# Two graph-convolution passes whose sum banks carry 128 columns into the next bank, instead of cutting tiles in two

## The reference: what is computed

```python
def gcn_conv(x, src, dst, ew, W, b):
    deg = segment_sum(ew, dst); dinv = where(deg > 0, rsqrt(deg), 0)
    h = x @ W
    msg = h[src] * (dinv[src] * ew * dinv[dst])[:, None]
    return segment_sum(msg, dst) + b
h = relu(gcn_conv(x, ..., W1, b1)); h = sigmoid(gcn_conv(h, ..., W2, b2))
x = layernorm(x + h)
z = x @ fc_w.T; rh = edge_attr @ fc_r_w.T
e = leaky_relu(z[src] @ aw0 + z[dst] @ aw1 + rh @ aw2)
alpha = segment_softmax(e, dst)
out = layernorm(x + relu(segment_sum(alpha * (z[src] + rh), dst) + z @ loop_w))
```

## Time and profile before

| what | value |
|---|---|
| median of 3 runs | 2682.67 us (2680.21 to 2683.11) |
| profiled execution | 2688.04 us, its span 2686.2 us |
| PE / DVE / ACT / POOL busy | 73% / 64% / 9% / 74% of the span |
| granted clock of PE, mean | 0.81 of full speed |
| pass 0 gathers | 5.7 to 843.1 us |
| pass 1 gathers | 856.5 to 1619.8 us |
| pass 2 gathers | 1646.3 to 2640 us |

### The profile page before, as it was taken

How to read it: one execution, slowest core, us unless ns; L and a number is a source line. 1 busy time by engine, 2 the same in 40 slices (tenths; PEclk the granted TensorE clock), 3 DMA queues, 4 the chain that set the end, 5 groups by cost and what they waited for, 6 DMA issues and landing times.

```text
span 2686.2 us, 39490 instructions
## 1 busy us (share of the span) xinstructions
PE 1962.5 (73%) x13505; PEld 1689.4 (63%) x13505; DVE 1731.3 (64%) x7072; ACT 253.3 (9%) x444; POOL 1998.3 (74%) x1973
## 2 busy tenths in 40 slices
PE   5777888989896787979797884466457566567558
PEld 4567767777785565757575763366456556456557
DVE  8989976867764456665656564556556457556465
ACT  0010000101100011101111111000000000000000
POOL 7777777777776777777777774777777777777772
PEclk9659888989986889889878885678788777788777
DMA  4243222222224233343424334644444444444441
GB/s 133 57 118 96 64 70 65 77 63 77 69 65 126 63 83 115 89 123 91 117 78 116 89 107 138 173 116 114 106 113 114 103 114 106 113 114 106 103 104 33
DMA packets 251443, 263.33 MB, mean 98 GB/s; under 512 B 41630, under 2 KB 195765, under 8 KB 251222
## 3 DMA queue, kind: packets, MB, share of 16 engines
q0 software_dynamic: 62784, 130.31, 19.8%
q1 hardware_dynamic: 175214, 123.97, 15.8%
q10 hardware_dynamic: 13240, 6.45, 0.8%
HBM read 247.25 MB, written 13.72 MB: 97 GB/s over the span
## 4 chain that ended last, share of the span: by engine, by line
POOL 45%; issue 19%; PE 16%; DVE 11%; DMA 7%; SPq 1%; ACT 0%; POOLq 0%; DVEq 0%; ACTq 0%
POOL ring L562 45%; PE ps L694 7%; DMA ring<-x_d,srcC 5%; DVE SR L1226 5%; PE ps L749 5%; DVE SR L1257 2%; PE ps L697 1%; DMA ring<-h_d,srcC 1%; PE ps L737 1%; DMA U<-dlo_d 1%; PE ps L679 1%; SPq L400 1%; SPq L482 1%; PE ps L634 0%; DVE SR L1323 0%
## 5 line engine op out<-in xcount | busy, mean ns | idle before, releaser
L562 POOL DMA_INDIRECT ring<-x_d,srcC x1260 | 1262.1, 1002 | 411.4 <-issue 395.2
L694 PE MATMUL ps<-SR,ring 128*128 128x128 f32 (+9 forms) x5076 | 904.3, 311 | 203.1 <-DVE SR L1257 75.3
L694 PEld LDWEIGHTS ps<-SR,ring 128*128 128x128 f32 x5076 | 797.9, 227 | 231.8 <-issue 140.5
L562 POOL DMA_INDIRECT ring<-h_d,srcC x558 | 593.5, 1064 | 183.1 <-issue 175.5
L749 PE MATMUL ps<-SR 128*128 128x376 f32 x1176 | 430.2, 518 | 33.6 <-ACT SR L989 33.6
L697 PE MATMUL ps<-SR 128*128 128x128 f32 (+10 forms) x1948 | 427.4, 305 | 0.0
L697 PEld LDWEIGHTS ps<-SR 128*128 128x128 f32 x1948 | 348.8, 224 | 0.0
L749 PEld LDWEIGHTS ps<-SR 128*128 128x128 f32 x1176 | 233.5, 207 | 176.1 <-ACT SR L989 35.4
L1323 DVE TENSOR_SCALAR SR<-iota_s,cols 128x376 f32<-128x376 f32 x588 | 246.7, 473 | 67.8 <-PE ps L749 67.5
L1257 DVE TENSOR_SCALAR SR<-iota_s,rankC,ewC 128x128 f32<-128x128 f32 x1036 | 280.0, 363 | 0.3
L829 PE MATMUL ps<-ident,cols 128*32 128x128 f32 (+2 forms) x78 | 20.4, 396 | 316.5 <-DVE cols L1533 316.5
(11 more groups left out here) (226 smaller groups left out, 1721.3 us busy)
## 6 DMA issues: line engine op xcount, KB each, us to landing
SR<-in_edge_attr_dram SPq DMA_DIRECT2D x97, 512.0 KB, 4.2
U<-dlo_d SPq DMA_DIRECT2D x98, 256.0 KB, 3.5
ring<-x_d,srcC POOLq DMA_INDIRECT x1260
SR<-low_d SPq DMA_DIRECT2D x72, 256.0 KB, 3.3
ring<-h_d,srcC POOLq DMA_INDIRECT x558
U<-lo_d SPq DMA_DIRECT2D x18, 256.0 KB, 3.2
x_d<-U SPq DMA_DIRECT2D x12, 264.0 KB, 4.5
rows<-x_d SPq DMA_DIRECT2D x12, 264.0 KB
```

What stands on the lines that cost most here:

```text
L562: pool.indirect_dma_start(ring[:, gg % R, k, 0:width], None, (x if p == 0 and h < R0 else table)[:, :], bass.IndirectOffsetOnAxis(ap=srcC[ ...
L694: last = nc.tensor.matmul(ps[(p * NK + k) % 2][:, lo:hi], ring[:, gg % R, j, 0:D], S[:, gg % NS, j, w0:w0 + hi - lo], start=False, stop=t ...
```

## The change

In passes 0 and 1 a bank now owns BA = 384 nodes (three blocks), and there are NA = 17 banks. A bank still has 512 columns. A tile is summed whole into the one bank that `bank_of` names, and columns 384 to 511 hold what its tiles add to the first 128 nodes of the next bank. When a bank has been copied to SBUF, `layer` first adds those 128 columns into the next bank, by one matmul with the identity, and then multiplies the bank's three blocks by the weights. The next bank's first tile is always the first tile of a group (`OPENS`); the last bank, which owns only block 48, is opened inside `layer`. Pass 2 keeps its 13 banks and `pieces`. The sets move to other banks and other groups: those that POOL leaves out in pass 0 were 42-45, 58-61, 74-77, 82-85, 90-93 and are now 44-47, 56-59, 74-77, 80-83, 92-95. Their number stays, as does the number of gathers in each pass.

The core of the diff; elsewhere `NK` becomes `NA`, `blocks(k)` becomes `home(k)` and `CLOSE` becomes `CLOSES` wherever passes 0 and 1 are meant, in the loads of `h1_d`, `x2_d` and `x` (17 smaller DMAs each instead of 13), in `hide`, `squash`, `hidden`, `hidden2`, `normal`, `dst_scores`, `node_table` and `picks_at`.

```diff
+BA = 3 * P
+NA = -(-NP // BA)
+def bank_of(t):
+    return max((GT * t - 2 * (W // 4)) // BA, 0) if t >= GT else 0
+def home(k):
+    return range(k * BA // P, min((k + 1) * BA // P, NB))
+def column(t):
+    return base(t) - bank_of(t) * BA
+OPENS = [min(t for t in range(T) if bank_of(t) == k) for k in range(NA)]
+CLOSES = [max(t for t in range(T) if bank_of(t) == k) // GT for k in range(NA)]
-SETK = (5, 7, 9, 10, 11, 1, 3)
+SETK = (7, 9, 12, 13, 15, 2, 4)
-SAT = [4 * k * P // GT + 16 for k in SETK]
+SAT = [OPENS[k] + GT for k in SETK]
...
 (sum_group)
+                    if p < 2:
+                        k = bank_of(t)
+                        if t == OPENS[k] and k + 1 < NA:
+                            open_bank(p, k)
+                        last = nc.tensor.matmul(ps[(p * NA + k) % 2][:, column(t):column(t) + W], ring[:, gg % R, j, 0:D], S[:, gg % NS, j, :],
+                                                start=False, stop=t + 1 in OPENS or t + 1 == T)
+                        continue
...
 (add_sets)
-                        at = base(SAT[RUNS[i]]) - k * BW
+                        at = column(SAT[RUNS[i]])
...
 (layer)
                 pe.wait_ge(s("evacd"), gb + 1)
+                if k + 2 == NA:
+                    open_bank(p, NA - 1)
+                if k + 1 < NA:
+                    nc.tensor.matmul(ps[(gb + 1) % 2][:, 0:BW - BA], ident[:, :], aggT[:, gb % 2, BA:BW], start=False, stop=False)
                 if gb:
                     pe.wait_ge(s("l_free"), gb)
-                for j, b in enumerate(blocks(k)):
+                for j, b in enumerate(home(k)):
...
 (evacuate)
-                n = len(blocks(k)) * P
+                n = BW if k + 1 < NA else len(home(k)) * P
```

More of the change, by code:

```diff
@@ L77 @@
 CLOSE = [t // GT for t in LAST[0]]
-SETK = (5, 7, 9, 10, 11, 1, 3)
+BA = 3 * P
[8 more added lines that the diff above has]
+CLOSES = [max(t for t in range(T) if bank_of(t) == k) // GT for k in range(NA)]
+assert all(0 <= column(t) and column(t) + W <= BW for t in range(T)) and all(OPENS[k] // GT == CLOSES[k - 1] + 1 for k in range(1, NA))
+SETK = (7, 9, 12, 13, 15, 2, 4)
 USED = ((0, 1, 2, 3, 4), (5, 6, 0, 1, 2, 3, 4))
@@ L90 @@
 SEQ = [(p, q) for p in range(3) for q in GL[p]]
-CLOSEH = [[GL[p].index(q) for q in CLOSE] for p in range(2)]
+CLOSEH = [[GL[p].index(q) for q in CLOSES] for p in range(2)]
 NC = -(-NB // 4)
@@ L94 @@
 NQ = 12
-assert all(base(t0) == GT * t0 - MARGIN and base(t0) // BW == (base(t0) + SPAN - 1) // BW == k for k, t0 in zip(SETK, SAT))
+assert all(bank_of(t0) == bank_of(t0 + ST - 1) == k and column(t0) + SPAN <= BW for k, t0 in zip(SETK, SAT))
 CUT = [[30, 39, 48, 57, 66], [1, 10, 19, 29, 38, 47, 57]]
@@ L121, in node_tiles @@
 def node_tiles(k):
-    return range(max(16 * blocks(k)[0] - 8, 0), min(16 * blocks(k)[-1] + 8, T) if k + 1 < NK else T)
+    return range(max(16 * home(k)[0] - 8, 0), min(16 * home(k)[-1] + 8, T) if k + 1 < NA else T)
 def picks_at(h):
@@ L129, in picks_at @@
     for i in range(h + 1):
-        ready = sum(len(node_tiles(k)) // GT for k in range(NK) if CLOSEH[1][k] + 4 <= i)
+        ready = sum(len(node_tiles(k)) // GT for k in range(NA) if CLOSEH[1][k] + 4 <= i)
         first, done = done, max(done, min(ready, done + 2))
@@ L434, in _ @@
             sp.wait_ge(s("looked"), N0 * NC)
-            for k in range(NK):
-                b0, b1_ = blocks(k)[0], blocks(k)[-1] + 1
+            for k in range(NA):
+                b0, b1_ = home(k)[0], home(k)[-1] + 1
                 sp.wait_ge(*stored(h1_stored, k))
@@ L773, in pick @@
                     pe.wait_ge(s("picked"), q - 1)
-                k = next(k for k in range(NK) if q * GT in node_tiles(k))
+                k = next(k for k in range(NA) if q * GT in node_tiles(k))
                 for j in range(GT):
@@ L799, in _ @@
                     sum_slots(m)
-                for k in range(NK):
-                    if CLOSEH[0][k] == (h if k == NK - 2 else h - 1):
+                for k in range(NA):
+                    if CLOSEH[0][k] == (h if k == NA - 2 else h - 1):
                         layer(0, k, w1)
-            layer(0, NK - 1, w1)
+            layer(0, NA - 1, w1)
             for h in range(HS[1]):
@@ L818, in _ @@
                     pick(q)
-            layer(1, NK - 1, w2)
-            for q in range(picks_at(HS[1] - 1)[-1] + 1, G):
+            layer(1, NA - 1, w2)
+            for q in range(picks_at(HS[1] - 1).stop, G):
                 pick(q)
@@ L1017, in _ @@
                         store_low(s_)
-                for k in range(NK - 2):
+                for k in range(NA - 2):
                     if CLOSEH[0][k] == h:
@@ L1038, in _ @@
                 set_copies(1, h)
-                for k in range(NK - 2):
+                for k in range(NA - 2):
                     if CLOSEH[1][k] == h:
                         evacuate(1, k)
-            for k in (NK - 2, NK - 1):
+            for k in (NA - 2, NA - 1):
                 evacuate(1, k)
@@ L1428, in node_table @@
                     dve.wait_ge(s("pick_summed"), node_tiles(k - 2)[-1] // GT + 1)
-                b0, b1_ = max(blocks(k)[0] - 1, 0), blocks(k)[-1]
+                b0, b1_ = max(home(k)[0] - 1, 0), home(k)[-1]
                 link(v.tensor_tensor(ds1[:, b0:b1_], s1n[:, b0 + 1:b1_ + 1], s1n[:, b0:b1_], ALU.subtract))
-                for b in range(b0, b1_ + (k + 1 == NK)):
+                for b in range(b0, b1_ + (k + 1 == NA)):
                     at = max(8 + 16 * b, 8)
@@ L1490, in _ @@
                 end_pick(q)
-            rest = picks_at(HS[1] - 1)[-1] + 1
-            for k in range(NK):
+            rest = picks_at(HS[1] - 1).stop
+            for k in range(NA):
                 if CLOSEH[1][k] > HS[1] - 4:
```

86 lines of the change are left out of this document (42 added, 44 removed).

## The result

The changed kernel takes **2666.93 us** (median of 5 runs, 2662.24 to 2672.92) where before takes 2682.67 us: a ratio of 0.995, with a 95% interval of 0.9932 to 0.9967. The two medians are 15.7 us apart, which alone would be 0.9941, inside that interval. It is faster by about half a per cent. The forecast was 2672 us, inside 2658 to 2683, and faster.

A forecast was written before the change was run, and what follows sets the result against it. POOL's three runs of gathers, two gaps between passes and a tail were taken to bound the kernel. 2688.0 - 3.4 - 7.0 = 2677.6 us, less 5.4 for the median, gave 2672 us, range 2658 to 2683.

The forecast's parts named there:

- The bound: Whole kernel: POOL's three runs of gathers, two gaps between passes and a tail make the time; PE counts only in gaps.
- PE's work in the body: Within passes 0 and 1: 704 records fewer, eight more clears, some 85 us off PE, almost none on the path.
- The end of pass 0: Gap before pass 1: first gather moves from 856.5 to 853.1, 3.4 us saved, bounds 1 and 6.
- The end of pass 1: Gap before pass 2: group 96 ends 10.7 us earlier, the way onward grows 3.6; 7.0 us saved, bounds 0 and 9.5.
- Pass 2 and the tail: Pass 2 and what follows its last gather: the same work on the same banks, only started earlier.
- Length of gathers: POOL's gathers: change taken as 0, bounds -55 to +27 us in pass 1, chance scatter 8 us.
- The clock gate: PE's clock: with less work PE waits more, so the clock may fall; ends already priced at the lower clock.
- (B): Rival in passes 0 and 1: DVE's runs fall across gathers and hold them longer; 2692 us at +20 us; chance 0.14.
- its mean clock lower: Sign that the forecast is right: PE's mean clock falls, along with 704 records of sums fewer; no size given.
- (C): Rival at the end of pass 1: bank 14's tail on DVE takes what PE wins, no gain there; 2679 us; chance 0.14.
- (D): Rival on gathers: DVE's runs fall better and the excess drops by 15 us; 2657 us; chance 0.12.
- (E): Rival for the whole kernel: PE is the bound after all and 85 us come off; 2598 us; chance 0.02.

The follow-up runs named there:

- e2: Kernel before, second matmul of tiles cut at the eleven borders other than the last left out in passes 0 and 1 (352 matmuls); 2678.23 us, ratio 0.9994.
- e1: Kernel before, second matmul of tiles cut at the last border left out in passes 0 and 1 (32 matmuls); 2669.06 us, ratio 0.9944.
- e7: The changed kernel again with no edit, its second profile; 2668.15 us, ratio 0.9949.
- e5: Changed kernel, with `end_pick` moved on DVE behind the one-hots of a step of pass 1; 2638.85 us, ratio 0.984.
- e9: Kernel before (13 banks), with `end_pick` moved behind the one-hots of a step of pass 1; 2647.85 us, ratio 0.9872.
- e6: Changed kernel with e3's and e5's edits, and the previous step's set one-hots spread between tile one-hots in passes 0 and 1; 2624.66 us, ratio 0.9792.
- e3: Changed kernel, with bank 14's `normal` and scores done earlier and its table after the last scores, at the end of pass 1; 2667.58 us, ratio 0.9938.
- e12: The changed kernel again with no edit, its third profile, a single execution; 2671.59 us.

## Why the prediction was right

**The bound.** Right. The time is three runs of gathers, two gaps and a tail; PE was relieved of over 100 us and the time followed the gaps. e2 shows the cover itself: 352 matmuls less, and no change.

**PE's work in the body.** Right in count (704 records, 8 clears), too small in time: 85 us were forecast; 107.5 were measured in this pair, and 103 between the means of four and three profiles (1958.0 and 1854.6 us), within which one kernel scatters by up to 23 us. That the price of a record was too low isn't seen: in its one profile, e2's 704 records took 86 us off, 0.122 us each. The granted clock is a little higher after the change (below), which may account for the rest; that isn't shown.

**The end of pass 0.** The sign and the place were right, and the term was mis-sized: 3.4 us forecast, 6.3 in this pair, 13.9 - 7.5 = 6.4 between the means. The step that failed is the pricing of everything "at the clock there", 0.22 us a record, and with it "so it does not hold this up" of group 97's last gather. The opening and group 91 did run at that clock (3.62 us for 16 records). From the carry on, PE ran at the full one: carry, layer and addition took 1.5 us, from 826.88 to 828.41, where 3.6 were forecast, and group 96 took 1.95 us, 0.122 a record, where 3.5 were. PE stood 3.8 us ahead of the issue of the last gather when group 96 ended (830.36 against 834.17), where 0.5 us were forecast and before was 3.7 us behind. From there on it is the gathers that are late: group 97 waits 1.42 and 0.92 us for its rows. What is left of the gap, 7.05 us, is a transfer and the way of the last block. The upper bound was 6 us, "if PE has caught up to the gathers before group 96". PE did wait for rows ahead of group 91 (5.46 us), but ran through group 96 without a wait and was stopped by the gathers only in group 97. In e1 group 96 ran at the lower clock (3.41 us for 16 records) and the gap is 7.55 us all the same: there two cut groups became whole ones, and no opening or carry was added. So a short gap here does not need the higher clock.

**The end of pass 1.** The lengths were close: the end of group 96 comes 13.3 us earlier against the last gather (10.7 forecast; 1597.29 against 1601.67, and 1628.67 against 1619.78 before), and the way from there is 20.6 us (21.2 forecast), with 4.6 us of DVE for bank 14 (4.7 forecast). The gap shrank by 10.2 us in this pair, and by 26.2 - 18.0 = 8.2 between the means, against 7.0 forecast. The step that failed is the same as in the first term: "near the late end, because the granted clock at this place is 0.55". It was 0.68 in the changed kernel. Group 91 took 3.62 us, the lower clock's time, but group 96 took 2.05 us, the full clock's, where a group at the lower clock takes 3.6. That is 1.5 of the 2.6 us by which group 96 ended earlier than forecast; how the rest divides isn't known, since 1618 was not a sum of priced steps. Against the gathers, group 96 ended where the forecast's earliest value, 1615.6, would have put it. In e7 it ended 4.4 us later against the gathers, and the gap there is 20.9 us.

**Pass 2 and the tail** stayed as forecast: 46.1 to 48.6 us of tail in the four profiles of before, 46.5 to 47.7 in the three of the change.

**Length of gathers.** "I take 0" holds within what can be measured. The chance scatter of 8 us is about what came: in four profiles of the kernel before the sum over passes 0 and 1 has a standard deviation of 7.9 us and ranges over 15. The 111 us that the prediction gives for the excess of these passes counts pass 0 from 300 us on; over all 1180 gathers it is 126.6 in the same profile, so its 127 us for a time slower than before would be some 143 in the table above.

**The clock gate.** The risk did not come. PE's busy share of the body fell from 472.49 / 526 = 90% to 438.18 / 520 = 84%, and the granted clock went from 0.92 to 0.93; the mean over the execution was 0.810 to 0.821 in four profiles of before and 0.822 to 0.825 in three of the change, where "its mean clock lower" was what would show. That sign did not come. As the prediction read the Trainium skill ("TensorE: Matmul & The Clock Gate", section "HAM oscillation — how this bites in real kernels"), waits between short bursts would let the clock fall; these runs do not show it at this level of work.

**The rivals.** (B) did not come: the excess did not grow, though a change of DVE's order can do such a thing, since the excess of pass 1 moves by 26 to 38 us in e5, e9 and e6, in the other direction. (C) is refuted by the second gap, though bank 14's tail does stand there, as e3 shows. (D) looked half true in the first pair and went away with more profiles. (E) is refuted by e2 and by idleness of 0.305 us a gather in both kernels. The sum came to 2672 against 2666.9 us: the gaps gave 14.6 us and not 10.4, and that is the difference, but for a microsecond that cannot be assigned.

## What to carry to other kernels

Where one engine is never short of work within a pass, as POOL here, look for the gain of another's removed work at the pass's ends: take the last few instructions before the drain, and price them apart, at both clock levels; here 32 matmuls out of 384 carried the gain. The share of an engine in the chain of waits is no measure of what relieving it gives. Compare several profiles of each kernel before a difference of 10 us in the sum of many small holds is given a cause.

## What the hardware showed that I had not expected

- The order of DVE's instructions alone, with the same instructions, moves the time by 1.3% (e9, 35 us), most of it through the length of POOL's gathers: the excess of pass 1 is 29 us below the mean of before, and the two gaps together are 11 us below it. On top of the change, e6's edits bring 43.5 us more (e7's 2668.15 to 2624.66), nearly three times what the change itself brings.
- A gather of 0.94 us can be held until an unbroken run of DVE ends (2.76 us in the example above). Of the 34 gathers over 1.5 us in pass 1 of the changed kernel, 20 end 0.10 to 0.14 us after such a run. It does not happen to every gather beside a run: 33 of the 38 that lie inside a run of over 1.5 us, and end while it goes on, last 0.94 to 1.25 us. What decides between them isn't shown. The Trainium skill ("SBUF — State Buffer", section "Who interferes with whom") has the loser blocked for a whole instruction; here POOL, where it was held, waited through several instructions that followed one another without a break.
- Tile one-hots, 128 columns wide, hold gathers less: in pass 1 they cover 3.5 us of the 64.0 us of excess with 17 gathers, although DVE is busy with either kind for some 145 us of the pass, while the set one-hots cover 47.3 us with 73 gathers. In pass 0 of the same kernel it is the other way round (17.2 us beside tile one-hots, 12.2 beside set one-hots), so this isn't a property of the width alone.
- The granted clock rose a little when PE was given less to do (0.55 to 0.68 at the end of pass 1). During group 96 it is 0.50, the level of 1.2 GHz, at both ends in three profiles of before, and 0.65 and 0.50 in the fourth; after the change it is 1.00, the level of 2.4 GHz, at five of six ends, and 0.83 at the sixth (e12, pass 1). Why isn't shown.
